# A transformer block on one core: a rearranged way into self-attention and another closing chain

## The reference, cut to what matters

```
x = x + cross_attention(layernorm(x), ctx_768)      # 32 x 32 queries of 512, 257 keys of 384 for each of 32 batches
x = x + self_attention(layernorm(x))                # 16 heads of 32, rotary, 32 tokens in each batch
x = x + moe(layernorm(x))                           # 8 experts of 512 -> 1024 -> 512, 2 for each token

self_attention: q = x@Wq.T + bq; k = x@Wk.T + bk; v = x@Wv.T + bv; rope(q), rope(k)
                softmax(q k / sqrt(32)) v @ Wo.T + bo
moe:            scores = sigmoid(x@gate.T + bias); top 2, scaled to a sum of 1
                out[t] = sum over the 2 experts e of score * (silu(x@w1[e].T) @ w2[e].T)
```

## Time and profile before

| | us |
|---|---|
| median of 3 runs | 543.81 (542.87 to 544.47) |
| profiled execution | 544.36 |
| its span, first to last instruction | 542.4 |
| outside the span | 1.96 |
| the chain of work that ended last, by engine | PE 64%, DVE 20%, DMA 5%, issue 3%, ACT 3%, POOL 2% |
| cross-attention up to its last context sums | 0 to 127 |
| the way in, to the first scores of self-attention | 127 to 160 |
| self-attention and routing | 160 to 284 |
| experts | 284 to 536 |

### The profile page before, as it was taken

The page is one execution under the profiler, slowest core; times in us unless marked ns, Lnnn a source line. Parts: engine busy times, 40 slices in busy tenths (PEclk is TensorE's granted clock), DMA queues, the critical chain, the costliest instruction groups (busy, mean ns, idle before and its releaser), DMA issues.

```text
span 542.4 us, 11280 instructions
## 1 busy us (share of the span) xinstructions
PE 489.0 (90%) x3722; PEld 281.0 (52%) x3723; DVE 378.4 (70%) x847; ACT 255.4 (47%) x397; POOL 113.3 (21%) x86
## 2 busy tenths in 40 slices
PE   3997999998988999975769899999999999999992
PEld 1743455555666676755555444445444454444541
DVE  3778897848979899898886877663746637673230
ACT  1313446555168385765642745544625445552220
POOL 0022212015050231300663022111121111221111
PEclk9999799999999999996968999999999999999997
DMA  8999578910009996166852589994895848743333
GB/s 296 406 398 366 174 292 325 407 49 1 1 1 351 381 381 228 40 232 211 293 201 83 152 268 256 287 246 126 226 241 141 248 112 233 232 75 61 58 58 40
DMA packets 55201, 110.95 MB, mean 205 GB/s; under 512 B 24416, under 2 KB 25600, under 8 KB 50048
## 3 DMA queue, kind: packets, MB, share of 16 engines
q1 hardware_dynamic: 25296, 87.80, 44.7%
q10 hardware_dynamic: 25568, 12.94, 10.1%
q0 software_dynamic: 4304, 9.77, 8.4%
HBM read 75.82 MB, written 29.43 MB: 194 GB/s over the span
## 4 chain that ended last, share of the span: by engine, by line
PE 64%; DVE 20%; DMA 5%; issue 3%; ACT 3%; SPq 2%; POOL 2%; DVEq 0%; ACTq 0%; POOLq 0%
PE bank L768 18%; PE bank L786 18%; PE bank L555 6%; PE bank L371 4%; DMA ctx_region<-in_ctx 4%; PE bank L539 3%; DVE wbuf L1590 2%; PE bank L520 2%; PE bank L581 2%; PE bank L469 2%; PE bank L750 1%; DVE small L1144 1%; DVE ctx_region L1387 1%; PE bank L515 1%; DVE small L1141 1%
## 5 line engine op out<-in xcount | busy, mean ns | idle before, releaser
L768 PE MATMUL bank<-wbuf,ctx_region 128*128 x480 | 108.2, 382 | 0.0
L1590 DVE SCALAR_TENSOR_TENSOR wbuf<-ctx_region,wbuf 128x2048 f32 (+1 forms) x28 | 62.9, 2288 | 30.4 <-ACT wbuf L953 29.0
L1821 POOL DMA_INDIRECT out<-misc,ints x21 | 39.7, 1892 | 205.1 <-ACT misc L1034 146.4
L768 PEld LDWEIGHTS bank<-wbuf,ctx_region 128*128 128x128 f16 x480 | 46.5, 99 | 53.0 <-issue 1.8
L953 ACT ACTIVATE wbuf<-ctx_region 128x2048 f32 (+1 forms) x28 | 52.0, 1904 | 27.8 <-issue 21.2
L1724 POOL TENSOR_TENSOR small<-small 128x2 f32<-128x2 f32 (+2 forms) x25 | 27.3, 1096 | 164.3 <-DVE small L1117 161.5
L786 PE MATMUL bank<-wbuf,actT 128*128 x264 | 58.8, 379 | 1.0 <-DVE actT L1681 1.0
L1053 ACT ACTIVATE ctxT_region<-bank 128x512 f32<-128x512 f32 x42 | 25.0, 597 | 69.2 <-PE bank L768 55.7
L786 PE MATMUL bank<-wbuf,xn 128*128 x240 | 53.4, 379 | 0.0
L555 PE MATMUL bank<-ctx_region,wbuf 128*128 128x256 f16 x384 | 43.3, 273 | 3.7 <-DVE ctx_region L1272 3.7
L786 PEld LDWEIGHTS bank<-wbuf,actT 128*128 128x128 f16 x264 | 25.8, 98 | 32.0 <-issue 1.2
(11 more groups left out here) (222 smaller groups left out, 800.0 us busy)
## 6 DMA issues: line engine op xcount, KB each, us to landing
ctx_region<-in_experts SPq DMA_DIRECT2D x28, 1024.0 KB
routed_rows<-ctxT_region SPq DMA_DIRECT2D x1, 16900.0 KB, 50.7
ctxT_region<-in_ctxT SPq DMA_DIRECT2D x8, 1542.0 KB, 11.8
ctx_region<-in_ctx SPq DMA_DIRECT2D x8, 1536.0 KB, 8.9
ctx_region<-routed_rows ACTq DMA_DIRECT2D x21, 260.0 KB, 3.2
wbuf<-in_experts SPq DMA_DIRECT2D x4, 1024.0 KB
out<-x ACTq DMA_DIRECT2D x8, 256.0 KB
wbuf<-in_wqT SPq DMA_DIRECT2D x4, 256.0 KB, 5.3
```

Of the source, the lines that this page charges most:

```text
L768: mm = nc.tensor.matmul(bank[half][:, :], xgT[:, b, x_part, k * P:(k + 1) * P], w16[:, ds(at + (w_part + k * EH + half * 512), 512)], star ...
L1590: nc.vector.scalar_tensor_tensor(w16[:, ds(at + (LOW + n * PIECE), PIECE)], src_[:, piece], W_SCALE, w16[:, ds(at + (HIGH + n * PIECE), PI ...
L1821: nc.gpsimd.indirect_dma_start(out, bass.IndirectOffsetOnAxis(idx[:, slot_no:slot_no + 1].bitcast(U32), axis=0), y_out[:, slot_no, :], Non ...
```

## The change

Four things are changed.

1. SP issues `swq` and `swk` in the turn of pair 1 (behind context tiles 4 and 5) and no longer in that of pair 2. `cut_self_high(0)`, `(1)`, `(2)` move to the turns of pairs 1, 2 and 3, each behind the exponentials. `cut_self_low(0)` and `(1)` move to the end of DVE's turn of pair 2, behind a wait for POOL's last context root.
2. `xnT` gets a second home in `shared` for the odd pairs (it lies over `cv` and `x2a`, so the first use waits for `y_ps`). ACT's `normalised_out(1)` moves ahead of `values_out(0)`, `cut_self_high(3)` ahead of the keys' bias. DVE centres the last context sums; `context_residual(3)` moves behind the first `turn`; `cut_self_low(3)` behind the first `join`. POOL does both layer norm roots first; `k_exp`'s memset waits for the third cut weight, `p_T`'s for the second `join`; the memset and copy in `xf` wait for all values.
3. In the loop DVE runs `first_scale` between `turn_cos` and `turn_sin` of the keys, and in pair 0 `attended_low` and `normalised_low` ahead of the queries' `turn_cos`.
4. The last tile's second product is made in two halves of 256 columns, in banks 5 and 7, each evicted for itself; its expert is looked up ahead of `hidden_T`. ACT and no longer POOL waits for the last store, and SP waits for both.

```diff
+        xnT_homes = (xnT, shared[:, 4 * ROW:4 * ROW + KC * 2 * P].bitcast(F16).rearrange(...))
@@ sync
-                if pair == 2:
+                if pair == 1:
                     sp.wait_ge(s["qkb_ps"], 1)
                     load_w(swq, "swqT", s["self_qk_in"])
                     load_w(swk, "swkT", s["self_qk_in"])
-            sp.wait_ge(s["finished"], 1)
+            sp.wait_ge(s["finished"], 2)
@@ tensor (by_channel and values read xnT_homes[pair % 2])
+            ready, at = experts_of(last)[0]
+            pe.wait_ge(s["w2_lo"], ready * 2)
             hidden_T(last)
-            second_product(last, 0, experts_of(last)[0])
+            pe.wait_ge(s["hT0"], last + 1)
+            pe.wait_ge(s["hT1"], last + 1)
+            for half in range(2):
+                for k in range(HC):
+                    for h_part, w_part in ((0, HIGH), (0, LOW), (1, HIGH)):
+                        column = w_part + W2_AT + k * D + half * (D // 2)
+                        mm = nc.tensor.matmul(bank[(5, 7)[half]][:, 0:D // 2], hT[0][:, h_part, k * P:(k + 1) * P],
+                                              w16[:, ds(at + column, D // 2)], start=..., stop=...)
+                mm.then_inc(s["y2_ps"], 1)
@@ scalar
             def normalised_out(pair):
+                if pair == 1:
+                    act.wait_ge(s["y_ps"], TILES)
...
-                if pair + 1 == PAIRS:
-                    cut_self_high(0)
+                if pair:
+                    cut_self_high(pair - 1)
...
-                else:
-                    cut_self_high(1)
...
-                for t in range(2):
-                    act.wait_ge(s["cv_raw"], 4 * pair + 2 * t + 2)
-                    scaled(cv[:, t, :], cv[:, t, :], 1.0, cv_shift[:, t:t + 1]).then_inc(s["cv"], 1)
                 if pair + 1 < PAIRS:
+                    for t in range(2):
+                        act.wait_ge(s["cv_raw"], 4 * pair + 2 * t + 2)
+                        scaled(cv[:, t, :], cv[:, t, :], 1.0, cv_shift[:, t:t + 1]).then_inc(s["cv"], 1)
...
-            cut_self_high(2)
...
             turned_out(0)
-            biased(k_T, 4, s["sk_ps"], 0, "sbk", s["sk"])
-            values_out(0)
-            normalised_out(1)
             act.wait_ge(s["sw_lo"], 3)
             cut_self_high(3)
-            act.wait_ge(s["ptx_zero"], 2)
+            biased(k_T, 4, s["sk_ps"], 0, "sbk", s["sk"])
+            normalised_out(1)
+            values_out(0)
+            act.wait_ge(s["ptx_zero"], 1)
             key_columns(0)
...
-            gated(last, 0)
+            act.wait_ge(s["gate"], last + 1)
+            act.wait_ge(s["added"], last + 1)
+            for half in range(2):
+                act.wait_ge(s["y2_ps"], last + (half + 1))
+                op = nc.scalar.activation(y_out[:, 0, half * (D // 2):(half + 1) * (D // 2)], bank[(5, 7)[half]][:, 0:D // 2],
+                                          ACT.Copy, scale=gates[:, 0, 2:3])
+            op.then_inc(s["y2"], 1)
+            act.wait_ge(s["scat"], last * 16 + 16)
+            act.sem_inc(s["finished"], 1)
@@ vector
+                if pair + 2 == PAIRS:
+                    dve.wait_ge(s["cx_rstd"], TILES)
+                    cut_self_low(0)
+                    cut_self_low(1)
...
+            def last_sums_centred(t):
+                dve.wait_ge(s["cv_raw"], 4 * (PAIRS - 1) + 2 * t + 2)
+                nc.vector.tensor_scalar(cv[:, t, :], cv[:, t, :], cv_shift[:, t:t + 1], None, ALU.add).then_inc(s["cv"], 1)
-            first_norm(0)
-            cut_self_low(0)
+            first_stats(0)
+            first_scale(0)
+            last_sums_centred(0)
+            first_stats(1)
+            last_sums_centred(1)
             normalised_low(0)
             sums_low(PAIRS - 1)
             dve.wait_ge(s["xnT_ps"], 2)
-            first_norm(1)
-            cut_self_low(1)
+            first_scale(1)
             dve.wait_ge(s["sw_lo"], 1)
             cut_self_low(2)
-            context_residual(PAIRS - 1)
...
             turn(0, 0)
+            context_residual(PAIRS - 1)
             join(0, 0)
-            turn(0, 1)
+            cut_self_low(3)
+            turn_cos(0, 1)
             normalised_low(1)
+            turn_sin(1)
             join(0, 1)
-            cut_self_low(3)
...
                 if not last:
-                    turn(pair + 1, 1)
-                    join(pair + 1, 1)
+                    turn_cos(pair + 1, 1)
                 if pair + 2 < PAIRS:
                     first_scale(pair + 2)
+                if not last:
+                    turn_sin(1)
+                    join(pair + 1, 1)
...
+                if pair == 0:
+                    attended_low(pair)
+                    normalised_low(pair + 2)
                 if pair + 2 < PAIRS:
                     turn_cos(pair + 1, 0)
...
@@ gpsimd
             inverse_root("ln3", 1, rstd, ve, 2)
+            inverse_root("ln3", 2, rstd, ve, 2)
             pool.wait_ge(s["cv_ps"], TILES)
+            pool.wait_ge(s["sw_lo"], 3)
             nc.gpsimd.memset(k_exp, 0.0).then_inc(s["ptx_zero"], 1)
-            inverse_root("ln3", 2, rstd, ve, 2)
-            nc.gpsimd.memset(p_T, 0.0).then_inc(s["ptx_zero"], 1)
...
             pool.wait_ge(s["rotated"], 2)
+            nc.gpsimd.memset(p_T, 0.0).then_inc(s["ptx_zero"], 1)
             plus_sbo(0)
...
                 if pair + 1 == PAIRS:
+                    pool.wait_ge(s["sv_ps"], TILES)
+                    nc.gpsimd.memset(xf[:, :, C_E2 + 1:ROW], 0.0).then_inc(s["rows_set"], 1)
...
-            pool.wait_ge(s["scat"], last * 16 + 16)
```

More of the change, by code:

```diff
@@ L547, in normalised_T, with by_channel @@
                     transposes(bank[t], [xn[:, t, k * P:(k + 1) * P] for k in range(KC)], s["xnT_ps"])
-            def by_channel(n, first, sem):
+            def by_channel(pair, n, first, sem):
                 pe.wait_ge(s["sw_lo"], n + 1)
@@ L555, in by_channel @@
                             mm = nc.tensor.matmul(bank[first + e // 2][:, e % 2 * 256:e % 2 * 256 + 256],
-                                                  w[w_part][:, k, e * P:(e + 1) * P], xnT[:, x_part, k, :],
+                                                  w[w_part][:, k, e * P:(e + 1) * P], xnT_homes[pair % 2][:, x_part, k, :],
                                                   start=(k == 0 and w_part + x_part == 0), stop=(k == KC - 1 and w_part == 1))
@@ L564, in queries @@
                     pe.wait_ge(s["cv"], TILES)
-                by_channel(0, 2, s["sq_ps"])
+                by_channel(pair, 0, 2, s["sq_ps"])
             def keys(pair):
-                by_channel(1, 4, s["sk_ps"])
+                by_channel(pair, 1, 4, s["sk_ps"])
             def values(pair):
@@ L580, in values @@
                         for x_part, w_part in PASSES:
-                            mm = nc.tensor.matmul(bank[6 + t][:, :], xnT[:, x_part, k, t * P:(t + 1) * P], swv16[w_part][:, k, :],
+                            mm = nc.tensor.matmul(bank[6 + t][:, :], xnT_homes[pair % 2][:, x_part, k, t * P:(t + 1) * P], swv16[w_part][:, k, :],
                                                   start=(k == 0 and x_part + w_part == 0), stop=(k == KC - 1 and x_part == 1))
@@ L801, in _ @@
                         second_product(i * 2 + (u - 1), (u - 1) % 2, experts[u - 1])
+            ready, at = experts_of(last)[0]
+            pe.wait_ge(s["w2_lo"], ready * 2)
             hidden_T(last)
-            second_product(last, 0, experts_of(last)[0])
+            pe.wait_ge(s["hT0"], last + 1)
[5 more added lines that the diff above has]
+                        mm = nc.tensor.matmul(bank[(5, 7)[half]][:, 0:D // 2], hT[0][:, h_part, k * P:(k + 1) * P],
+                                              w16[:, ds(at + column, D // 2)],
+                                              start=(k == 0 and h_part + w_part == 0), stop=(k == HC - 1 and h_part == 1))
+                mm.then_inc(s["y2_ps"], 1)
         @block.scalar
@@ L859, in normalised_out @@
             def normalised_out(pair):
+                if pair == 1:
+                    act.wait_ge(s["y_ps"], TILES)
                 for t in range(2):
                     act.wait_ge(s["xnT_ps"], 2 * pair + t + 1)
-                    nc.scalar.copy(xnT[:, 0, :, t * P:(t + 1) * P],
+                    nc.scalar.copy(xnT_homes[pair % 2][:, 0, :, t * P:(t + 1) * P],
                                    bank[t][:, :].rearrange("p (k t) -> p k t", k=KC)).then_inc(s["xnT"], 1)
@@ L1262, in first_scale @@
                 dve.wait_ge(s["ln3_out"], 2 * pair + 2)
-            def first_norm(pair):
-                first_stats(pair)
-                first_scale(pair)
             def normalised_low(pair):
@@ L1271, in normalised_low @@
                     tile_at = slice(t * P, (t + 1) * P)
-                    nc.vector.tensor_tensor(xnT[:, 1, :, tile_at], bank[t][:, :].rearrange("p (k t) -> p k t", k=KC),
```

(9 more changed lines are left out.)

5 lines of the change are left out of this document (3 added, 2 removed).

## The result

The changed kernel takes **537.84 us** (median of 6 runs, 536.98 to 539.71); the kernel before, measured beside it, 543.61 (6 runs, 542.45 to 544.47). The profiled execution took 536.98, its span 534.4.

The account below looks back on a forecast made before the run. PE, busy 90% of the span, was the bound, so only its idle stretches could yield time. 0.3 + 2.7 + 0.45 + 0.2 = 3.6 us took 544.36 to 540.8, on the median 540.3 us; 8-in-10 range 538.7 to 542.3.

Parts of the forecast that it names:

- the halves: Last tile's product in two halves: eviction ends some 0.6 us sooner, gaining nothing as the last store waits for another store.
- the hand-over: Program's end: ACT in place of POOL waits for the last store; between nothing and 2.9 us saved, taken as 0.2.
- the loop: DVE's new order in pair 0 of the loop: of PE's 2.6 us of holes, 0.45 us kept.
- the way in: Phase up to `scores(0)`: it starts at 156.6 us instead of 159.60, 3.0 us earlier.
- most of the 2.9 at the end: Rival, more gain than counted: most of this time at the program's end, or PE's full 2.6 us, saved; 538.2 us, 8%.
- The earlier look-up: Last tile's expert looked up ahead of `hidden_T`: no gain; price none, at most 1.0 us idle before the last product.
- The two meet: Ahead of `scores(0)`: ACT ends the key columns at 156.5 us and PE ends `queries(1)` at 156.45, so it starts at 156.6.
- Pair 0: First loop turn: two PE holes (1.41, 1.25 us) go, PE then waits 1.6 us; `scores(1)` 187.4 for 188.2, softmax gains 0.5.
- The load: Rival, way in: `swk` landing at 83.7 us stalls ACT's cut and PE stands 5.5 us; 545.8 us, 4%.
- The additions: Rival, way in: POOL's four additions collide with DVE's softmax, up to 1.3 us lost; 541.7 us, 9%.
- The shift given back: Rival, after the way in: DVE and DMA chains between 230 and 300 us, or a slower clock, undo gains; 543.3 us, 9%.

Follow-up runs that it names:

- wait_only: Kernel before with one edit: ACT, no longer POOL, waits for the last store's landing, and SP waits for both: 541.19 us for 543.4, ratio 0.9963.
- both_wait: Kernel before, but ACT waits for the last store and tells SP; POOL waits last for the same landing, telling nobody: 543.89 us for 543.38, ratio 1.0013.
- one_home: Whole change, but `xnT` has one home and ACT makes `values_out(0)` ahead of `normalised_out(1)`: 541.39 us for 543.82 of the kernel before, ratio 0.9959.
- way_only: Whole change without part 4, the closing chain: 538.64 us, ratio 0.9912 to the kernel before.
- early_memsets: Whole change, but POOL makes both memsets one after the other right behind the cross-attention: 536.87 us for 543.82 of the kernel before, ratio 0.9888.
- attended_first: Whole change, with `attended_low` and `normalised_low` ahead of the queries' `turn_cos` in pair 1 too: 536.26 us for 543.38 of the kernel before, ratio 0.9876.

## Why the prediction was wrong

Every gain but that of the halves was looked for where it came; the sum failed on sizes, all on one side. Against 3.6 us: the hand-over 1.6 to 1.7 for 0.2, the loop 0.86 for 0.45, the halves 0.2 for nothing, the way in 3.06 for 3.0. These make the missing 2.1 to 2.2.

**The step that failed: "No row shows the hand-over... so I take 0.2."** Its ends, nothing and 2.9, were right, and the value was taken from "single POOL queue entries on the chain take 0.02 to 0.05 us". But those rows are of POOL in the middle of its work, and they were not even all of it. The chain of before, ahead of the last store, has 0.53 us of "issue" between two such entries:

```profile
533.46 0.02 POOLq L1820
533.47 0.53 issue
534.00 0.04 POOLq L1831
```

From that landing (533.43) to the store POOL took 0.8 us. And the cost lies at POOL's end, where the trace of before shows only 2.9 us without a name. `wait_only` gives 1.6 to 1.7 for this edit alone (6.46 us for 8.03 and 8.17), and `both_wait` takes it away again by giving POOL the late wait. With ends so far apart the middle, 1.4, and a wider range would have been right: with 1.4 the sum gives 539.1. The same mechanism stood among the rivals as "most of the 2.9 at the end", 538.2 with 8%. That was the nearest to what happened.

**The halves.** I had them gain nothing, since the last store waited for the store before until 533.43, and for the eviction only until 533.24. A lead of 0.2 us in one execution decides nothing. In the six other profiles with the whole product ACT's eviction released the last store, 5.99 to 6.00 us behind the one before; with the halves it is 5.77 to 5.81. So they give 0.2. In five of the six profiles with halves ACT's eviction is still what releases the store. I had put the eviction's end 0.6 us sooner; it came 0.2 sooner, 5.94 us behind the start of the last product for 6.16. The earlier look-up gave nothing: PE stands 1.04 us for DVE ahead of that product before and after. First before, then after:

```profile
527.08 5.35 PE L786 MATMUL bank<-wbuf,actT 128*128 x24 [1.04 <-DVE actT L1681]
```
```profile
521.09 5.43 PE L812 MATMUL bank<-wbuf,actT 128*128 x48 [1.04 <-DVE actT L1714]
```

ACT's evictions after:

```profile
524.02 0.47 ACT L1110 ACTIVATE misc<-bank,small 128x256 f32<-128x256 f32 x1 [2.78 <-PE bank L812]
526.56 0.47 ACT L1110 ACTIVATE misc<-bank,small 128x256 f32<-128x256 f32 x1 [2.06 <-PE bank L812]
```

**Way in.** Forecast `scores(0)` 3.0 earlier, measured 3.06, and `one_home` shows that the second home carries it. Its inner terms were less good. `queries(0)` gained 0.59 for 0.3: `context_result(2)` was 0.17 late (2.91 us behind sc(3) for 2.74), as forecast, the centring took 0.42 for my 0.4, and the low part began 15.47 us behind sc(3), where my own times put it at 15.75, the 0.2 included. PE followed 0.06 us behind its end, as before, so the 0.3 that I had missed are the low part's. I had set DVE's rows end to end, and neighbouring ones overlap by 0.08 us in the trace: the centring at 123.97 ends at 124.39, the statistics begin at 124.31.

```profile
123.97 0.42 DVE L1378 TENSOR_SCALAR shared<-shared,small 128x384 f32<-128x384 f32 x1
...
126.31 1.28 DVE L1288 TENSOR_TENSOR ctx_region<-bank,ctx_region 128x512 f16<-128x512 f32 x2
```

What `queries(0)` gained beyond the forecast did not reach `scores(0)`, since the key columns are late next, by 0.31 in the row at 154.63. "The two meet" was right.

**Pair 0.** `queries(2)` came 2.5 us nearer to `scores(0)`, as forecast, and DVE's join is the wait behind it. The join ended 27.4 us behind `scores(0)`, exactly as before, where I had let it come 0.3 later: in both orders DVE does the same work there without a pause. So `scores(1)` gained 1.18 for 0.8. The softmax gained 0.88 (it starts 28.88 us behind `scores(0)`, in the earlier trace rows 29.76) for 0.5: `last_scale`, the bound, ends just ahead of it in the row at 182.59. `scores(2)` gives 0.32 back, where I had 0.35; the rest, 0.9, is whole at `scores(3)`.

**The rivals.** *The load*: it did not strike. Issue to landing was 13.7 us, as in the old row of 13.9. In the changed kernel SP issued `swk` at 60.19, it landed at 73.9, and ACT cut at 74.40 without idling. In `way_only` SP's issue of the context tiles ahead of it took 4.69 us for 2.64, `swk` was issued at 63.07, and ACT waited for it; the query rows came right behind the cut, and PE took them at 83.36 without a hole. Counted from ACT's exponentials just ahead (74.08 before, 72.66 and 73.17 in these two), the landings are at 75.3 and 77.8 on the time axis of before, on either side of my 76.5 and far from the 83.7. The 0.42 MB/us that I took is near what the engines moved in their fullest stretches before: 416 GB/s from 86 to 90 us and 436 from 98 to 102. ACT in `way_only`:

```profile
76.92 1.91 ACT L875 ACTIVATE wbuf<-wbuf 128x2048 f16<-128x2048 f32 x1 [1.91 <-DMA wbuf<-in_swkT]
78.82 1.93 ACT L823 ACTIVATE shared<-bank,cols 128x256 f32<-128x256 f32 x4
```

*The additions*: 4.96 us for four, 1.24 each and so undisturbed (1.26 in the earlier trace rows), ended at 158.7, 0.7 ahead of the softmax's first product of two SBUF inputs at 159.43; the softmax's steps on DVE beside them, from 155.77 on, took 0.68 to 0.69 us each. *The shift given back*: from s(2) to the last but one store before took 311.16, after 311.01; beyond the 0.32 above, nothing is seen to be given back, as far as a phase can tell that wanders by 2 us. That phase holds one visit of the slower clock in either: at the earlier trace rows's 310.72 before, where 24 matmuls took 6.52 us (granted clock 0.80 from 310.7 to 317.2 us) and 5.18 later in the same chain, and at 231 after. Where it did not come at either place (`way_only`, `early_memsets`, `attended_first`) the phase took 309.5, in `wait_only` 308.6; that last 0.9 us lies between `scores(3)` and the first product of the experts, and its cause is not known.

## What to carry to other kernels

What stands between the last landing and the end of the program belongs in the sum as a term with a range of its own; try another engine for the last wait, and here let POOL's last wait be one that is fulfilled early. A release by two events within 0.2 us of each other in one profile is to be counted as a tie, with both outcomes in the range. When an order is changed to remove a hole, look for the resource that keeps two pieces of work apart (here one home of a tile): with a second home the new order gained 3.1 us, with one it lost 0.7. Follow a gain past the next step before counting it: the 0.4 us of `attended_first` were gone one pair later.

## What the runs showed of the hardware

- POOL as the last engine to be released costs some 1.6 us at the program's end: 8.03 to 8.38 us from the last store to the end with POOL's late wait, be it for a DMA or for ACT, and 6.45 to 6.62 without, in every profile.
- A memset of POOL that only writes SBUF held a layer norm on DVE (`early_memsets`: 6.16 us for 1.00), and two memsets one behind the other let nothing of it in between: its first instruction, begun at 129.3, ended at 135.0, behind the second memset's end at 134.75.
- The start of a span is chance of 1 to 3 us: the first tile of x landed at 9.9 us in the profile before and at 7.75 in the profile after, with the same code. Two profiles' spans should be compared by phases: here they differ by 8.0, where the medians differ by 5.8.
- The slower clock comes at changing places in the same code. At the end of pair 2 a visit costs 1.7 us (26.77 after for 25.08 in `way_only`; granted clock 0.62 from 231 to 235 us after, 1.00 in `early_memsets`), in the expert loop 1.3 (24 matmuls before in 6.52 us for 5.18; clock 0.80 from 310.7 to 317.2 us). In the context sums of pair 0 five of the profiles have one (2.79 us for 1.50 in the second sums, with a granted clock of 0.50 from 59 to 62.5 us); at most 0.5 us of it is left at sc(3), which comes 56.3 to 56.8 us behind the start of these sums with and without it.
